# Spiral scan and two attentions on one core: queries projected once and copied, the shift turned by one product, split scan levels with one step product

## The reference, cut to what matters

```
neigh = mean of the (up to 4) neighbours, as they are now
y     = tanh(concat(local, neigh) @ w1 + b1) @ w2 + b2      # w1: 256 x 256, w2: 256
local = local + y * w_y                                      # w_y: 128
```

```
q, k, v = x @ Wq + bq, x @ Wk + bk, x @ Wv + bv              # 16, 16 and 128 columns
out     = softmax(q k^T) v  (times gamma in layer 1)  + x
```

## Time and profile before

| | us |
|---|---|
| median of 3 runs | 4900.87 (4898.67 to 4903.14) |
| profiled execution, its own time | 4921.94 |
| its span | 4920.0 |

### The profile page before, as it was taken

The page is one execution under the profiler, slowest core; times in us unless marked ns, Lnnn a source line. Parts: engine busy times, 40 slices in busy tenths (PEclk is TensorE's granted clock), DMA queues, the critical chain, the costliest instruction groups (busy, mean ns, idle before and its releaser), DMA issues.

```text
span 4920.0 us, 58630 instructions
## 1 busy us (share of the span) xinstructions
PE 4626.7 (94%) x17960; PEld 2484.7 (51%) x17960; DVE 3785.9 (77%) x7132; ACT 2869.6 (58%) x5225; POOL 2307.7 (47%) x4230
## 2 busy tenths in 40 slices
PE   6997996999999999999999999999999998997996
PEld 2454754455555555555555555555555553444754
DVE  4885876788888778887788788888787885885876
ACT  1222321777777777777777777777777773222322
POOL 3453431455555555555555555555555555453431
PEclk8998998899999999999999999999999999998998
DMA  6677636011111111111111111111111413596836
GB/s 127 69 78 84 105 52 60 26 43 43 43 41 41 39 43 43 43 44 43 43 42 39 42 43 43 44 43 43 43 39 39 98 39 77 49 94 78 102 64 43
DMA packets 471719, 273.28 MB, mean 56 GB/s; under 512 B 437360, under 2 KB 438640, under 8 KB 471408
## 3 DMA queue, kind: packets, MB, share of 16 engines
q1 hardware_dynamic: 471408, 269.54, 29.9%
HBM read 135.29 MB, written 134.22 MB: 55 GB/s over the span
## 4 chain that ended last, share of the span: by engine, by line
PE 67%; POOL 12%; DVE 8%; issue 6%; DMA 3%; SPq 2%; ACT 1%; DVEq 0%; POOLq 0%; ACTq 0%
PE psum L953 15%; PE psum L896 8%; PE psum L887 7%; PE psum L877 7%; PE psum L925 6%; PE psum L983 6%; PE psum L961 4%; PE psum L959 4%; PE psum L958 4%; POOL probs_low L534 3%; PE psum L1011 3%; PE psum L938 3%; PE psum L972 3%; DVE x L774 2%; SPq L402 2%
## 5 line engine op out<-in xcount | busy, mean ns | idle before, releaser
L534 POOL TENSOR_TENSOR probs_low<-shared,probs_high 128x512 fp32r<-128x512 f32 x1024 | 1308.8, 1278 | 1430.6 <-DVE probs_high L755 1430.6
L717 DVE TENSOR_REDUCE top<-psum 128x1 f32<-128x1024 f32 x1024 | 1253.6, 1224 | 572.0 <-PE psum L938 571.6
L823 ACT ACTIVATE shared<-psum 128x512 f32<-128x512 f32 x2048 | 1110.1, 595 | 383.7 <-PE psum L925 375.9
L828 ACT ACTIVATE psum<-psum,top 128x1024 f32<-128x1024 f32 x1024 | 1112.9, 1087 | 368.5 <-DVE top L717 368.5
L813 ACT ACTIVATE shared<-psum,b_col 128x320 f32<-128x320 f32 (+10 forms) x744 | 413.0, 566 | 1164.8 <-PE psum L887 1150.3
L953 PE MATMUL psum<-shared 128*128 128x512 f32 x2048 | 1087.8, 613 | 1.1 <-issue 0.7
L525 POOL TENSOR_TENSOR shared<-arena 128x32 f32<-128x32 f32 (+6 forms) x1230 | 564.7, 490 | 940.7 <-PE psum L887 763.8
L958 PE MATMUL psum<-probs_high,v_high 128*128 128x512 f32 x1024 | 813.9, 795 | 0.0
L887 PE MATMUL psum<-shared,w_sum 128*128 128x320 f32 (+10 forms) x1488 | 533.4, 481 | 126.2 <-DVE shared L680 90.5
L877 PE MATMUL psum<-arena,w_own 128*128 128x320 f32 (+12 forms) x1672 | 528.0, 443 | 31.0 <-DMA arena<-x_cells 29.0
L896 PE MATMUL psum<-shared,w2wy 128*128 128x320 f32 (+10 forms) x1488 | 519.8, 472 | 14.3 <-ACT shared L813 7.8
(11 more groups left out here) (74 smaller groups left out, 4934.0 us busy)
## 6 DMA issues: line engine op xcount, KB each, us to landing
x<-layer_out SPq DMA_DIRECT2D x128, 512.0 KB, 3.3
layer_out<-x SPq DMA_DIRECT2D x128, 512.0 KB, 2.6
arena<-x_cells SPq DMA_DIRECT2D x8, 1520.0 KB, 11.1
layer_out<-arena SPq DMA_DIRECT2D x8, 1520.0 KB, 21.1
arena<-layer_out SPq DMA_DIRECT2D x8, 1520.0 KB, 11.0
y_cells<-arena SPq DMA_DIRECT2D x8, 1520.0 KB, 22.2
arena<-x_cells SPq DMA_DIRECT2D x4, 1504.0 KB, 19.0
layer_out<-arena SPq DMA_DIRECT2D x4, 1504.0 KB, 19.3
```

The costliest lines, as they stand in the source:

```text
L534: nc.gpsimd.tensor_tensor(probs_low[n % 2][:], probs[u % PROBS], probs_high[n % 2][:], ALU.subtract).then_inc(probs_split, 1)
L717: nc.vector.reduce_max(top[i % 2][:, m:m + 1], rows_ps[m % 2][:], AX_X, negate=True).then_inc(row_max, 1)
L823: nc.scalar.activation(probs[u % PROBS], keys_ps[u % 2], ACT.Exp).then_inc(probs_ready, 1)
L828: nc.scalar.activation(rows_ps[m % 2][:], rows_ps[m % 2][:], ACT.Exp, bias=top[i % 2][:, m:m + 1], accum_out=total[i % 2][:, m:m + 1]).the ...
```

## The change

1. `WINDOW` goes from 432 to 462 columns. By the kernel's own placing, chunk 5 now has a place of its own and is loaded at the start too; chunk 6 follows after level 13, chunk 7 after level 26, chunk 8 after 33, chunk 9 after 40, chunk 10 after 49.
2. Queries are projected once, as the keys are (two products with 64 output rows, the two halves of the cells in the two row groups). VectorE splits them once, and SyncE copies each half across to the other row group by two DMAs (`swap_queries`), so that group 1 holds the halves in the other order (`queries_at`).
3. The shift is turned by one product with 16 output rows (`turn_shift`), copied to SBUF by VectorE (`take_shift`), stored to DRAM and read back into the two spare rows of each row group by three DMAs (`store_shift`, `place_shift`). `log_sums` has twelve operations, and runs at step 2, behind `split_probs` of that step.
4. The steps of the software pipeline shift: row energies run three steps earlier, projections of keys and queries are at steps 6 and 7 for job j+3, values at steps 1 and 3, the loop starts one job earlier.
5. In the split levels, ScalarE weighs the first tanh half by w2 in place between the two tanh (Copy with a scale), VectorE adds the second half weighed by w2 (`weigh`), and TensorE does one step product with `wy_rows` instead of two. `add_steps` is gone there: `update` comes first, and `new_sums` reads the updated cells. TensorE's order becomes steps A, near B, own A, steps B, near A, own B.

```diff
-WINDOW = 5 * CHUNK - 48
+WINDOW = 5 * CHUNK - 18
...
+def queries_at(g, h):
+
+    return h if g == 0 else 1 - h
...
+        def swap_queries(i):
+            if is_job(i):
+                sp.wait_ge(q_ready, i + 1)
+                for g in range(2):
+                    sp.dma_start(q[i % 3][ROW_GROUPS[g], half(1)].bitcast(F32),
+                                 q[i % 3][ROW_GROUPS[1 - g], half(0)].bitcast(F32)).then_inc(q_swapped[i % 2], 16)
+        def store_shift(i):
+            if is_job(i):
+                sp.wait_ge(shift_turned, i + 1)
+                positive(sp, shift_placed[i % 2], 48 * (i // 2))
+                sp.dma_start(shift_row[i % 2].rearrange("a (m p) -> (a m) p", p=P), turned[i % 2][:]
+                             ).then_inc(shift_stored[i % 2], 16)
+        def place_shift(i):
+            if is_job(i):
+                sp.wait_ge(shift_stored[i % 2], 16 * (i // 2 + 1))
+                for g, h in ((0, None), (1, 0), (1, 1)):
+                    ...
+                    sp.dma_start(q[i % 3][rows, ...].bitcast(F32),
+                                 shift_row[i % 2][:, cells_of]).then_inc(shift_placed[i % 2], 16)
...
-            for j in range(-3, JOBS + 1):
+            for j in range(-4, JOBS + 1):
                 for s in range(MT):
                     if s == 2:
                         store_image(j - 1)
-                    if s == 4:
+                    if s == 3:
                         load_image(j + 3)
+                    if s == 5:
+                        store_shift(j + 1)
+                    if s == 6:
+                        place_shift(j + 1)
+                    if s == 7:
+                        swap_queries(j + 3)
...
                 split_probs(j, 2 * s + 1)
-                if s == 5:
+                if s == 2:
                     log_sums(j + 1)
...
+        def weigh(n, c, lv):
+            dve.wait_ge(tanh_ready[c], levels_done(n, c, lv) * HALVES)
+            dve.wait_ge(weighed_first[c], levels_done(n, c, lv))
+            nc.vector.scalar_tensor_tensor(cells(hidden[0], c, lv), cells(hidden[1], c, lv), w2_col[n][:, 1:2],
+                                           cells(hidden[0], c, lv), ALU.mult, ALU.add).then_inc(weighed[c], 1)
...
                 for c in (A, B):
-                    add_steps(n, c, lv + 1)
                     update(n, c, lv)
+                    new_sums(n, c, lv + 1)
+                    weigh(n, B if c == A else A, lv if c == A else lv + 1)
                     if lv + 2 < JOIN:
-                        sums(n, c, lv + 2)
+                        old_sums(n, c, lv + 2)
...
+        def take_shift(i):
+            if is_job(i):
+                dve.wait_ge(shift_rows, i + 1)
+                positive(dve, shift_stored[i % 2], 16 * (i // 2))
+                nc.vector.tensor_copy(turned[i % 2][:], misc_ps[0:2 * MT, 0:P]).then_inc(shift_turned, 1)
...
# VectorE's attention(j, s)
-            row_maximum(j + 1 + (s + 3) // MT, (s + 3) % MT)
+            row_maximum(j + 1 + (s + 6) // MT, (s + 6) % MT)
+            if s == 2:
+                guess_log(j + 1)
+            if s == 3:
+                low_values(j + 1)
             if s == 5:
-                guess_log(j + 1)
...
+                take_shift(j + 1)
+            if s == 6:
+                split_keys(j + 3)
             if s == 7:
...
+                split_queries(j + 3)
             round_probs(j, 2 * s + 1)
...
# ScalarE's squash(n, c, lv)
+                if h == 0 and c != BOTH:
+                    act.wait_ge(tanh_ready[c], levels_done(n, c, lv) * HALVES - 1)
+                    nc.scalar.activation(cells(hidden[0], c, lv), cells(hidden[0], c, lv), ACT.Copy,
+                                         scale=w2_col[n][:, 0:1]).then_inc(weighed_first[c], 1)
...
# TensorE's steps(n, c, lv) and scan(n)
             if c != BOTH:
                 positive(pe, updated[c], levels_done(n, c, lv - 1))
+                pe.wait_ge(weighed[c], levels_done(n, c, lv))
+                nc.tensor.matmul(columns(step(c, lv), c, lv), wy_rows[n][:], cells(hidden[0], c, lv),
+                                 start=True, stop=True).then_inc(step_ready[c], 1)
+                return
...
+                steps(n, A, lv)
+                near_products(n, B, lv)
+                if lv + 1 < JOIN:
+                    own_products(n, A, lv + 1)
+                steps(n, B, lv)
+                if lv + 1 < JOIN:
+                    near_products(n, A, lv + 1)
+                    own_products(n, B, lv + 1)
...
# TensorE's key_energies, project_queries, turn_shift and attention(j, s)
-            if n == 0:
-                pe.wait_ge(shift_placed, 2 * i + h + 1)
+            if u == 0:
+                pe.wait_ge(shift_placed[i % 2], 48 * (i // 2 + 1))
...
+            pe.wait_ge(k_ready, i + 1)
+            for g in range(2):
+                mm = nc.tensor.matmul(misc_ps[ROW_GROUPS[g], :], wq_rows[job_layer(i)][:], x[i % DEEP][:, half(g)],
+                                      start=True, stop=True)
+            mm.then_inc(q_raw, 1)
...
+            nc.tensor.matmul(misc_ps[0:2 * MT, 0:P], shift[i % 2][:], ident_r[:], start=True, stop=True
+                             ).then_inc(shift_rows, 1)
...
+            row_energies(j + 1 + (s + 6) // MT, (s + 6) % MT)
+            if s in (1, 3):
+                project_values(j + 1, s // 2)
+            if s == 5:
+                turn_shift(j + 1)
+            if s == 6:
+                project_keys(j + 3)
             if s == 7:
-                spread_shift(j + 1, 0)
+                project_queries(j + 3)
```

More of the change, by code:

```diff
@@ L244, in turn_count @@
 def turn_count(n, c, lv):
-    per = [len(SUMS_OLD[v]) + len(SUMS_NEW[v]) + len(EDGES[v]) + step_turns(c, v) for v in SPAN[c]]
+    per = [len(SUMS_OLD[v]) + len(SUMS_NEW[v]) + len(EDGES[v]) + (step_turns(c, v) if c == BOTH else 0)
+           for v in SPAN[c]]
     return n * sum(per) + sum(per[:lv - SPAN[c].start])
@@ L308, in network @@
              [t[f"L2_conv_{w}"] for w in ("wq", "bq", "wk", "bk", "wv", "bv")]]
+    shift_row = [nc.dram_tensor(f"shift_row{n}", [2, CELLS], F32, kind="Internal").ap() for n in range(2)]
     arena = sb("arena", [P, BATCH, ARENA])
@@ L318, in network @@
     w2wy = [[sb(f"w2wy{n}_{h}", [P, P]) for h in range(HALVES)] for n in range(2)]
+    wy_rows = [sb(f"wy_rows{n}", [P, P]) for n in range(2)]
     wy_col = [sb(f"wy_col{n}", [P, 1]) for n in range(2)]
@@ L323, in network @@
     q = [sb(f"q{n}", [P, CELLS], F32R) for n in range(3)]
-    k = [sb(f"k{n}", [P, BANK], F32R) for n in range(3)]
+    k = [sb(f"k{n}", [P, BANK], F32R) for n in range(DEEP)]
     v = [shared[n][:, half(0)] for n in range(2)]
@@ L336, in network @@
                                                    ("ratio", "excess", "square", "slope", "bend", "log_sum"))
-    shift = [sb(f"shift{n}", [P, 2, STRIP], F32R) for n in range(2)]
-    wq_rows = [sb(f"wq_rows{n}", [P, P]) for n in range(LAYERS)]
+    shift = [sb(f"shift{n}", [P, 2 * MT], F32R) for n in range(2)]
+    turned = [sb(f"turned{n}", [2 * MT, P]) for n in range(2)]
+    wq_rows = [sb(f"wq_rows{n}", [P, ROW_GROUP]) for n in range(LAYERS)]
     wk_rows = [sb(f"wk_rows{n}", [P, ROW_GROUP]) for n in range(LAYERS)]
@@ L541, in log_sums @@
             s, y, e = total[i % 2], guess[i % 2], shrink[i % 2]
-            first, second = (shift[i % 2][:, :, r + TOP_ROW:r + TOP_ROW + MT].rearrange("p h (m a) -> p h m a", a=2)
-                             for r in (0, ROW_GROUP))
-            value = ratio[:].rearrange("p (h m) -> p h m", h=2)
+            high, low = shift[i % 2][:, 0:MT], shift[i % 2][:, MT:2 * MT]
             turn = LOG_TURNS * i
@@ L581, in _ @@
         scan(0)
-        for j in range(-2, JOBS + 1):
+        for j in range(-3, JOBS + 1):
             for s in range(MT):
                 split_probs(j, 2 * s + 1)
-                if s == 5:
+                if s == 2:
                     log_sums(j + 1)
```

172 lines of the change are left out of this document (73 added, 99 removed).

## The result

The changed kernel takes 4813.74 us (median of 4 runs, 4810.14 to 4814.45), the kernel before beside it 4902.01: ratio 0.9819, 95% interval 0.9805 to 0.9834, 88 us faster. The forecast of 4751 was 63 us too low, 62 in the change and 1 in the median of before that it started from (4900.87); the range held it. The profiled execution took 4813.82 us, 108 less than that of before (4921.94), which was itself 20 us above its unprofiled runs.

The account below looks back on a forecast made before the run. TensorE, busy 94%, was taken as the bound, with latency setting the new split levels. From 4921.94 us: -138 + 5 + 54 - 76 + 5 = -150, so 4772; from the median 4900.87, 4751 us; range 4620 to 4845.

Parts of the forecast that it names:

- The attention's products: Attention job: queries 1.01 us in place of 1.70, values and keys unchanged; TensorE's own work 23.27 us, 1.92 less.
- the turn: Attention: one product turning the shift in place of eight that cost 1.36 us; bounds 0 and 0.3, 0.13 taken.
- The new wait: Attention, low product of unit 7 in step 4: TensorE waits 0.84 us a job for GpSimd's split; bounds 0 and 1.5.
- The rival without this wait: Attention: VectorE may round earlier, so no new wait; 107 us less, 4644; chance 0.13.
- The load of image j+3: Attention, SyncE's queue: lands some 3 us after a store ending 5.9 us into the job, read at 17 us: hidden.
- The shift through DRAM: Attention: trip done 7.2 us after step 5's start, needed by the next job's keys at 9.4: hidden, 2.2 to spare.
- The slower rival: First key product of each job: shift late through DRAM, slower than before from 3.4 us above the sum; 5020, chance 0.07.
- The split levels: Both scans: latency sets periods of 5.05, 4.40, 3.37 us at 16, 13, 8 cells; +54 us for both scans.
- The chunk: Level 36 of each scan: chunk 7 loads earlier, so the wait and slow products after it go; -76 us.
- Start and ends: First scan's start: chunk 5 loaded early, +5 us; attention's start: one more projection round, +5, bounds 0 and 12.
- The median: Whole kernel: median of runs lies 21 us below the profiled execution, and that difference is taken over to the forecast.

Follow-up runs that it names:

- e1: Changed kernel with GpSimd's twelve small operations cut in two, the last four moved to step 3 behind unit 7's split: 4691.96 us, ratio 0.9549.
- e2: Changed kernel with the seven loads of cells for the second scan issued one a job over seven jobs: 4796.11 us, ratio 0.9759.
- e4: Changed kernel with the window of cells 432 wide again in place of 462: 4845.13 us, ratio 0.9872.
- e7: Changed kernel with four more stores of the shift to DRAM in each job, each waited for before the placing DMAs: 5068.39 us, one execution.
- e3: Changed kernel with the split levels of both scans as in the kernel before: 4781.29 us, ratio 0.9730.
- e5: Changed kernel without ScalarE's weighing Copy; VectorE adds the second tanh half times w2_1/w2_0 to the unweighed first: 4720.78 us, ratio 0.9615.
- e0: The kernel before, unchanged, profiled a second time: 4913.08 us, beside nine runs with a median of 4914.37.

## Why the prediction was right, and where 62 us went

The direction and the mechanisms held; the size was too large by 42 us in the sum (-150 against -108) and by another 20 in carrying it to the median.

- **The attention's products: right but for the turn.** Queries at 1.01 us, values and keys unchanged. "One is bounded by 0 and 0.3, and I take 0.13": it is 0.25. That is 15 us over 128 jobs. The row of L1075 has 0.23 for the product alone, inside the bounds, and the middle was the wrong pick: a single product isn't an eighth of eight in a row (before, four in a row took 0.50, and 0.40 of the 1.36 was the wait for GpSimd).
- **The new wait: right in place and cause, 0.18 us too small.** "8.65 - 7.81 = 0.84"; it costs 1.02, 23 us in all. From step 2's start, 2007.78, the product was wanted at +7.81 as predicted (2015.36 and the 0.23 that elsewhere lie between those two starts) and began at +8.73, 0.08 later than worked out, since the chain of twelve took 3.62 us (2011.57 to 2015.19) against 3.55. The other 0.10 is between it and the next key product: 0.43 us behind a wait, 0.33 otherwise. e1 shows that the chain in front of the split is all of it. The rival without this wait (4644) was wrong for this order, but one edit away.
- **The load of image j+3: the step that failed.** "Lands some 3 us later ... and is read at step 6, 17 us into the job: hidden." That holds for 127 jobs. The working priced the queue of a steady job; behind job 116 seven loads stand on it for 28.8 us. It cost 27 us, shown by e2. The burst stood in the code and in the trace of before; that it cost nothing there was due to its place, right behind an image load with free time after it, and to a cover of five steps. The change took both: its orders of the shift and of the queries went ahead of the burst, and the cover became three steps. e4 has the six loads of before behind the new orders, and its job 117 is still some 22 us too long.
- **The shift through DRAM: right, with too much caution.** The trip was put at 7.2 us after step 5's start; it is 2020.53 + 2.02 - 2016.94 = 5.6. Its store releases the next DMA after 1.38 us where I took 2.0. The page "DMA: Bandwidth & Descriptors" of the Trainium skill (section "Anatomy of one DMA") gives about 2.0 as the fixed cost. Its section is on DMAs that GpSimd issues, and these are SyncE's: neither leg agrees with it. The store releases its successor after 1.38 us, and the last of the three placing DMAs, issued 0.57 us behind the first, has landed 1.45 us later. Nor did the 2.60 us of the 512 KB store agree, as the prediction says: by the page's 2.0 us and 436 GB/s that store takes 3.2, an estimate. The cover was right: 5.6 and the slack of 3.7 from e7 make 9.3 where 9.4 was predicted. The slower rival asked for 3.4 us more than my sum; e7 had to add 5.4.
- **The split levels: right.** Period 5.05, 4.40, 3.37 predicted; 5.19, 4.37, 3.18 found; +54 predicted, +44 found; e3 has 44 by the ratios and 40 in its trace. Small errors cancel: `weigh` takes 0.99 and not 0.75 at 16 cells, but 0.48 and not 0.55 at 8, and the handovers, 0.47 in the prediction, add up to 0.44 from its own terms (0.20 and three times 0.08), 8 us over 256 periods. e5 shows the Copy to be on the path.
- **The chunk: right.** -76 predicted, -77 found, plus about 6 at chunk 5 that no step had. By e3 and e4 it hangs on the window alone.
- **Start and ends.** First scan's start +6.4 for +5. The attention's start is 3.4 us longer (from its first key projection to its first key product), where I had +5; its end and the 14 shorter jobs give 8 back, which no step had. The whole levels, +7.4 together, were in no step. They belong to the window: with 432 (e4) they are 3.2 us shorter in each scan, as before, and with the old split levels (e3) they are only 0.2 and 1.1 shorter. Why a wider window slows them no run shows.
- **The median.** "I take the difference over": e0 shows that an execution's distance to its median is not a constant of the kernel. The changed kernel's execution had none (4813.82 beside 4813.74), and the 20 us went with it. Taking the difference over was the error.

The terms: 23 + 15 + 27 + 7 = 72 too hopeful, 10 (split levels), 6 (chunk 5), 10 (ends) and some 4 of smaller ones too careful; 42 are left, and 20 from the median.

## What to carry to other kernels

When orders are added to an in-order queue or moved in it, look through the whole program for the one place where that queue holds something large, and ask what now stands ahead of it and what waits behind it: cover that is ample in 127 iterations decides in the 128th. Operations that an engine does in order are best split at the point where another engine wants a result; here one `if s == 3` was worth 132 us, more than the whole change. A product saved in a chain that isn't bound by products is paid back in latency: price the chain, not the engine.

## What the runs showed that I had not expected

- **A cast and a GpSimd operation exclude each other.** The cast of 0.42 us that began at 2015.42, inside GpSimd's split (2015.19 to 2016.46), ended at 2016.75, 0.29 behind it; GpSimd's L597, begun 0.01 us ahead of a cast, took 0.48 instead of 0.20. The cast's mean was 526 ns in the changed kernel and 416 in e1, where no cast falls into a split of that step. The page "SBUF — State Buffer" of the Trainium skill (section "SBUF: two separate sides") says that the port pair which the two share is an exclusive lock, held for the whole instruction by the one that starts first, where VectorE's is of a kind that takes both of its pairs. By that rule the first row agrees. The second doesn't: by the record GpSimd's started first, and it waited; in 110 of the 111 long cases it did so, 0.007 to 0.016 us ahead of the cast.
- **A DMA's issue is cheap alone and dear in a burst.** A load of 1520 KB holds SyncE for 0.43 us alone (e2). In the row of seven the first takes 0.60 us and the others up to 5.86, 28.77 in all; the store of 512 KB behind them took 5.71 us to issue, 0.34 otherwise.
